# Feed-forward of a quantised transformer block: the transposes of x and h move from TensorE and ScalarE to transposing DMAs on SyncE's queue

## The reference, cut to what matters

```python
def fp4_quant_dequant(x):
    xb = x.reshape(shape[:-1] + (shape[-1] // 16, 16))
    scale = jnp.maximum(jnp.max(jnp.abs(xb), -1, keepdims=True) / 6.0, 1e-12)
    xn = xb / scale
    idx = jnp.searchsorted(_MID, jnp.abs(xn))
    return (_GRID[idx] * jnp.sign(xn) * scale).reshape(shape)

def fp4_linear(x, w):
    return jnp.einsum('bsk,nk->bsn', fp4_quant_dequant(x), fp4_quant_dequant(w))

h = _layernorm(x) * (1 + cb) + sb
gate, y = fp4_linear(h, w_gate), fp4_linear(h, w_up)       # 512 -> 1408
x = x + gb * fp4_linear(silu(gate) * y, w_down)            # 1408 -> 512
```

## Time and profile before

| | |
|---|---|
| median of 3 runs (lowest, highest) | 4354.51 us (4353.13, 4363.64) |
| profiled execution, first to last instruction (span) | 4344.3 us |
| feed-forward's tiles in it, about | 2807 to 4344 us |
| PE busy, whole span | 3769.6 us, 87% |
| DVE busy, whole span | 3500.5 us, 81% |
| ACT, POOL busy | 1612.9 and 1139.1 us |

### The profile page before, as it was taken

One profiled execution on the slowest core, in us unless ns is written; L12 is line 12 of the kernel. 1 busy time (PEld: TensorE's weight loads), 2 busy tenths in 40 slices (PEclk: granted clock), 3 DMA queues, 4 the chain that ended last, 5 costly groups with the idle time before them and its releaser, 6 DMA issues. The chain is left out here.

```text
span 4344.3 us, 155632 instructions
## 1 busy us (share of the span) xinstructions
PE 3769.6 (87%) x65992; PEld 2590.6 (60%) x65992; DVE 3500.5 (81%) x7798; ACT 1612.9 (37%) x3173; POOL 1139.1 (26%) x736
## 2 busy tenths in 40 slices
PE   4888898888898888888888874399999999999999
PEld 3767777676677766777767652145454545545454
DVE  4777788777688776778777757799999999999997
ACT  2434434344353443443434313233333333333333
POOL 1121112211212212112121104433333333333332
PEclk7999999999899998999999986599999999999999
DMA  3000000000000000000000011001111111111100
GB/s 112 13 22 27 23 28 18 23 27 18 23 27 23 27 22 19 27 18 33 18 23 27 13 71 66 15 23 37 31 37 35 33 38 30 37 32 36 38 30 30
DMA packets 73617, 133.45 MB, mean 31 GB/s; under 512 B 13248, under 2 KB 14016, under 8 KB 72896
## 3 DMA queue, kind: packets, MB, share of 16 engines
q1 hardware_dynamic: 72896, 123.13, 8.8%
HBM read 89.56 MB, written 33.55 MB: 28 GB/s over the span
## 5 line engine op out<-in xcount | busy, mean ns | idle before, releaser
L747 POOL TENSOR_TENSOR raw_up<-raw_up,raw_gate 128x1024 f32<-128x1024 f32 x128 | 309.8, 2420 | 1184.1 <-DVE raw_up L797 1184.1
L915 DVE COPY_PREDICATED Am<-pick,banks 128x64 f32<-128x64 uint8 (+2 forms) x1792 | 460.6, 257 | 128.3 <-DVE Am L915 12.6
L1630 PE MATMUL fbank<-dT,hqT 128*128 128x512 f16 x2112 | 490.3, 381 | 21.1 <-ACT hqT L1547 21.1
L1618 PE MATMUL fbank<-gT,xqT 128*128 128x464 f16 (+1 forms) x2304 | 490.1, 363 | 11.4 <-issue 6.6
L1618 PE MATMUL fbank<-uT,xqT 128*128 128x464 f16 (+1 forms) x2304 | 488.3, 362 | 0.0
L526 PE MATMUL banks<-raw_up,raw_gate 128*128 128x256 f32 x2048 | 465.8, 386 | 6.2 <-issue 4.4
L526 PEld LDWEIGHTS banks<-raw_up,raw_gate 128*128 128x128 f32 x2048 | 391.0, 193 | 61.0 <-issue 7.0
L758 POOL TENSOR_TENSOR yrs<-yvar,neg_half 128x32 f32<-128x32 f32 x32 | 174.0, 5437 | 846.0 <-DVE yvar L944 846.0
L1618 PEld LDWEIGHTS fbank<-gT,xqT 128*128 128x128 f16 x2304 | 225.3, 98 | 247.7 <-issue 11.5
L1558 ACT ACTIVATE sil<-fbank,und 128x464 f32<-128x464 f32 (+1 forms) x192 | 124.0, 646 | 656.0 <-PE fbank L1618 656.0
L1618 PEld LDWEIGHTS fbank<-uT,xqT 128*128 128x128 f16 x2304 | 225.6, 98 | 231.7 <-issue 1.3
(11 more groups left out here) (235 smaller groups left out, 8063.1 us busy)
## 6 DMA issues: line engine op xcount, KB each, us to landing
raw_scale<-in_L_attn_x SPq DMA_DIRECT2D x32, 512.0 KB, 3.8
xres<-in_L_attn_x SPq DMA_DIRECT2D x32, 512.0 KB, 3.5
x_after_attention<-xres SPq DMA_DIRECT2D x32, 512.0 KB, 3.6
xl<-x_after_attention SPq DMA_DIRECT2D x64, 256.0 KB, 2.7
xr<-x_after_attention SPq DMA_DIRECT2D x64, 256.0 KB, 2.7
out<-xr SPq DMA_DIRECT2D x64, 256.0 KB, 2.0
raw_gate<-in_L_ffn_w_gate SPq DMA_DIRECT2D x1, 2816.0 KB, 11.5
raw_up<-in_L_ffn_w_up SPq DMA_DIRECT2D x1, 2816.0 KB, 18.7
```

Of the source, the lines that this page charges most:

```text
L747: nc.gpsimd.tensor_tensor(xf[:, j % NXF].rearrange("p g b t -> p (g b) t"), xf[:, j % NXF].rearrange("p g b t -> p (g b) t"), hT[:, :, :, ...
L915: nc.vector.copy_predicated(dst, mask, src).then_inc((done or A_step).sem, 1)
L1618: last = nc.tensor.matmul(GU[2 * pair + t][:, 0:w], xqT[:, u, a, g, :], W[:, b_, g, lo_:hi_], start=(k == 0), stop=(k == 3 * G - 1))
L1630: last = nc.tensor.matmul(DN[1 - u][:], hqT[:, a, kk, :], dT[:, b_, kk, :], start=(first and kk == 0), stop=(end and kk == KF - 1))
```

## The change

The transposes on PE and the copies on ACT go away, with their two PSUM banks. In their place SP issues three transposing DMAs for a tile, from SBUF to SBUF: one for xq (both parts, 128x1024 fp16), one for the high part of hq (128x1408) and one for its low part. hqT gets a second buffer. In SP's stream of body n, the loads of xl (n+2) and xr (n) come first, then the DMA of xq of tile n+1, the two of hq of tile n, and then the store of tile n-1. The down matmuls run in one piece: 22 after the high part has landed, 11 after the low part. The `sem_inc` on turn_go ahead of each DMA carries the wait; nothing waits for turn_go.

```diff
@@ -1337,7 +1336,7 @@
         xq = sb("xq", [P, 2, C], F16)
         hq = sb("hq", [P, 2, I_FF], F16)
         xqT = sb("xqT", [P, 2, 2, G, P], F16)
-        hqT = sb("hqT", [P, 2, KF, P], F16)
+        hqT = sb("hqT", [P, 2, 2, KF, P], F16)
         sil = sb("sil", [P, 2, 480])
         h = sb("h", [P, 2, I_FF])
         mh = sb("mh", [P, I_FF])
...
@@ -1355,8 +1354,9 @@
         Q_STEPS, Q_SCALED = 12, 4
         xgrid_done, hgrid_done = sig("xgrid_done", 1), sig("hgrid_done", 1)
         xlow_done, hlow_done = sig("xlow_done", 1), sig("hlow_done", 1)
-        xT_done, xT_used = sig("xT_done", 1), sig("xT_used", 1)
-        hT_done, hT_used = sig("hTf_done", 4), sig("hTf_used", 4)
+        xT_landed = sig("xT_landed", 1, 16)
+        hT_high, hT_low = sig("hT_high", 1, 16), sig("hT_low", 1, 16)
+        turn_go = sig("turn_go", 3)
         gu_done, sil_done, h_done = sig("gu_done", 3), sig("sil_done", 3), sig("h_done", 3)
         und_done = sig("und_done", 1)
         down_done = sig("down_done", 1)
...
@@ -1417,8 +1417,24 @@
         xstep.per, hstep.per = Q_STEPS, Q_STEPS
 
 
-        def sp_body(sp, j, u, n, do_m, do_out, more):
-            if more:
+        def sp_xT(sp, u, n):
+            after(sp, xq_done, n)
+            after(sp, xlow_done, n)
+            after(sp, gu_done, n - 2)
+            sp.sem_inc(turn_go.sem, 1)
+            sp.dma_start_transpose(xqT[:, u].rearrange("p a g t -> p (a g) t"), xq[:].rearrange("p a n -> p (a n)")).then_inc(xT_landed.sem, 16)
+
+        def sp_hT(sp, u, n):
+            after(sp, hq_done, n)
+            after(sp, down_done, n - 2)
+            sp.sem_inc(turn_go.sem, 1)
+            sp.dma_start_transpose(hqT[:, u, 0], hq[:, 0]).then_inc(hT_high.sem, 16)
+            after(sp, hlow_done, n)
+            sp.sem_inc(turn_go.sem, 1)
+            sp.dma_start_transpose(hqT[:, u, 1], hq[:, 1]).then_inc(hT_low.sem, 16)
+
+        def sp_body(sp, j, u, n, do_m, do_out, more, loads):
+            if loads:
                 after(sp, ln_done, n)
                 b, ts_ = tile_of(j + 1, u)
                 sp.dma_start(xl[:, u], x1[b, ts_, :]).then_inc(xl_loaded[u].sem, 16)
...
@@ -1426,6 +1442,10 @@
                 after(sp, out_stored[u], j - 1)
                 b, ts_ = tile_of(j, u)
                 sp.dma_start(xr[:, u], x1[b, ts_, :]).then_inc(xr_loaded[u].sem, 16)
+            if more:
+                sp_xT(sp, 1 - u, n + 1)
+            if do_m:
+                sp_hT(sp, u, n)
             if do_out:
                 after(sp, out_done, n - 1)
                 jj = j if u else j - 1
...
@@ -1460,7 +1480,7 @@
 
         def dve_hq(dve, u, n):
             after(dve, h_done, n)
-            quantise(dve, n, I_FF, h[:, u], mh[:], q16h, sh, ih, s16h, hp[:, u], hstep, hgrid_done, hq, hq_done, lambda: after(dve, hT_done, n - 1),
+            quantise(dve, n, I_FF, h[:, u], mh[:], q16h, sh, ih, s16h, hp[:, u], hstep, hgrid_done, hq, hq_done, lambda: (after(dve, hT_high, n - 1), after(dve, hT_low, n - 1)),
                      lambda: after(dve, hlow_done, n - 1))
 
         def dve_out(dve, j, u, n):
...
@@ -1558,49 +1560,11 @@
                     nc.scalar.activation(sil[:, pair, 0:hi_ - lo_], GU[2 * pair][:, 0:hi_ - lo_], ACT.Silu, scale=und[:, u, 0:1]).then_inc(sil_done.sem, 1)
                     if s == 0 and more:
                         act_grid(act, n + 1, xstep, hx[:], mx[:], xgrid_done)
-            if do_out:
-                act_hT(act, n - 1, 0)
-                act_hT(act, n - 1, 1, u)
-            if more:
-                act_xT(act, 1 - u, n + 1)
-            if do_out:
-                act_hT(act, n - 1, 2)
             if two_more(n):
                 act_ln(act, u, n + 2)
-            if do_out:
-                act_hT(act, n - 1, 3)
             if do_m:
                 act_grid(act, n, hstep, h[:, u], mh[:], hgrid_done)
...
@@ -1608,7 +1572,7 @@
                     pair = (3 * u + s) % 2
                     w = hi_ - lo_
                     if s == 0:
-                        after(pe, xT_used, n)
+                        after(pe, xT_landed, n)
 
                     after(pe, h_done, n if s >= 2 else n - 1, s - 1 if s >= 2 else s + 2)
                     for t, W in ((0, gT), (1, uT)):
...
@@ -1620,30 +1584,18 @@
                                 k += 1
                     last.then_inc(gu_done.sem, 1)
             if do_out:
-                m = n - 1
-                pe_hT(pe, m, 0, None)
-                pe_hT(pe, m, 1, None, u)
-                if more:
-                    pe_xT(pe, 1 - u, n + 1)
-                def down(ks, a, b_, first=False, end=False):
-                    for kk in ks:
-                        last = nc.tensor.matmul(DN[1 - u][:], hqT[:, a, kk, :], dT[:, b_, kk, :], start=(first and kk == 0), stop=(end and kk == KF - 1))
+                m, v = n - 1, 1 - u
+
+                def down(a, b_, first=False, end=False):
+                    for kk in range(KF):
+                        last = nc.tensor.matmul(DN[v][:], hqT[:, v, a, kk, :], dT[:, b_, kk, :], start=(first and kk == 0), stop=(end and kk == KF - 1))
                     return last
-                after(pe, hT_used, m, 1)
-                down(range(4), 0, 0, first=True)
-                after(pe, hT_used, m, 2)
-                down(range(4, 8), 0, 0)
-                pe_hT(pe, m, 2, None)
-                down(range(8), 0, 1)
-                pe_hT(pe, m, 3, n + 1 if more else (n if do_m else m))
-                after(pe, hT_used, m, 3)
-                down(range(8), 1, 0)
-                after(pe, hT_used, m)
-                down(range(8, KF), 0, 0)
-                down(range(8, KF), 0, 1)
-                down(range(8, KF), 1, 0, end=True).then_inc(down_done.sem, 1)
-            elif more:
-                pe_xT(pe, 1 - u, n + 1)
+                after(pe, hT_high, m)
+                after(pe, scaled_out, m - 2)
+                down(0, 0, first=True)
+                down(0, 1)
+                after(pe, hT_low, m)
+                down(1, 0, end=True).then_inc(down_done.sem, 1)
 
         def run(eng, body, first=None):
 
```

More of the change, by code:

```diff
@@ L1325, in feed_forward @@
         GU = bank[0:4]
-        TR = bank[4:6]
         DN = bank[6:8]
@@ L1449, in dve_xq @@
             after(dve, mod2, n)
-            quantise(dve, n, C, hx[:], mx[:], q16x, sx, ix, s16x, xp[:, u], xstep, xgrid_done, xq, xq_done, lambda: after(dve, xT_done, n - 1),
+            quantise(dve, n, C, hx[:], mx[:], q16x, sx, ix, s16x, xp[:, u], xstep, xgrid_done, xq, xq_done, lambda: after(dve, xT_landed, n - 1),
                      lambda: after(dve, xlow_done, n - 1),
@@ L1505, in pool_xlow @@
         def pool_xlow(pool, n):
-            low_part(pool, n, C, q16x, s16x, xq_done, xq, xlow_done, lambda: after(pool, xT_done, n - 1))
+            low_part(pool, n, C, q16x, s16x, xq_done, xq, xlow_done, lambda: after(pool, xT_landed, n - 1))
         def pool_body(pool, j, u, n, do_m, do_out, more):
@@ L1513, in pool_body @@
             if do_m:
-                low_part(pool, n, I_FF, q16h, s16h, hq_done, hq, hlow_done, lambda: after(pool, hT_done, n - 1))
+                low_part(pool, n, I_FF, q16h, s16h, hq_done, hq, hlow_done, lambda: after(pool, hT_low, n - 1))
             if do_out:
@@ L1529, in act_grid @@
             nc.scalar.activation(m, src, ACT.Abs, bias=grid_shift[:], scale=GRID_SCALE).then_inc(done.sem, 1)
[L1531 to L1547, removed]
         def act_body(act, j, u, n, do_m, do_out, more):
@@ L1622, in pe_body @@
             if do_out:
-                m = n - 1
-                pe_hT(pe, m, 0, None)
-                pe_hT(pe, m, 1, None, u)
-                if more:
-                    pe_xT(pe, 1 - u, n + 1)
-                def down(ks, a, b_, first=False, end=False):
-                    for kk in ks:
-                        last = nc.tensor.matmul(DN[1 - u][:], hqT[:, a, kk, :], dT[:, b_, kk, :], start=(first and kk == 0), stop=(end and kk == KF - 1))
-                    return last
-                after(pe, hT_used, m, 1)
-                down(range(4), 0, 0, first=True)
-                after(pe, hT_used, m, 2)
-                down(range(4, 8), 0, 0)
-                pe_hT(pe, m, 2, None)
-                down(range(8), 0, 1)
-                pe_hT(pe, m, 3, n + 1 if more else (n if do_m else m))
-                after(pe, hT_used, m, 3)
-                down(range(8), 1, 0)
-                after(pe, hT_used, m)
-                down(range(8, KF), 0, 0)
-                down(range(8, KF), 0, 1)
-                down(range(8, KF), 1, 0, end=True).then_inc(down_done.sem, 1)
-            elif more:
-                pe_xT(pe, 1 - u, n + 1)
+                m, v = n - 1, 1 - u
+                def down(a, b_, first=False, end=False):
+                    for kk in range(KF):
+                        last = nc.tensor.matmul(DN[v][:], hqT[:, v, a, kk, :], dT[:, b_, kk, :], start=(first and kk == 0), stop=(end and kk == KF - 1))
+                    return last
```

(9 more changed lines are left out.)

## The result

The changed kernel takes 4303.7 us (median of 7 runs, 4298.6 to 4329.9), the kernel before 4353.1 in the runs beside it. The ratio is 0.9907, interval 0.988 to 0.9935: 0.9% faster, where the prediction said 1.9% slower. It is the first rival, *hidden*, which had a chance of 0.31; the time lies between its two figures (4333 us, and 4279 us if POOL's operations cost DVE nothing). The profiled execution's span is 4301.5 us, 42.8 less than before.

The account below looks back on a forecast made before the run. PE was taken as the bound by a little, DVE right behind. A loss of 1.65 less a gain of 0.42 gives 1.23 us a tile, 76 us over 62 tiles, plus 5 at the ends: 4435 us, range 4285 to 4885.

Parts of the forecast that it names:

- the first rival, *hidden: On SP's queue: L below 2.7 us, xl in time, DVE the bound; 4333 us, or 4279; chance 0.31.
- I take half, 3.5 us: Estimate of L for one part of hq, half of the 7.1 us upper figure; the lower was 2.1 us.
- L: Time from when SP can issue one hq part's transposing DMA until what stands behind it can go; taken as 3.5 us.
- the place where L is paid: SP's queue between hq and xl's load: DVE's statistics wait for xl, 1.65 us a tile.
- The cover of all other DMAs: Before the down matmuls: hq's high part has 9.5 us for 3.5 and a landing, xq 9.3 for 2.6 and a landing.
- DVE stands right behind PE: Feed-forward tile of 23.57 us: PE busy 23.24, DVE 22.27, so taking 2.2 us from PE can't give 2.2.
- the norm's place on ACT: Without the copies ahead, ACT's norm of tile n+2 starts about 3 us earlier, as do POOL's two operations that delay DVE.
- The gain by position: On DVE: POOL's two operations move from L1397 and L1398 to beside L1386 and L1390; 0.42 us a tile, all told.
- the silu's wait: DVE waits 0.16 us for PE's silu of slice 2; claimed as the direct gain of relieving PE.
- The slack of xl: Between xl's landing and DVE's statistics: 1.5 us before the change, used up at L = 2.7 us.
- The prediction's formula: On SP's queue: xl's slack is used up when 3217.05 + 2L + 3.4 passes 3225.80.
- The ends: First transposes of x become a DMA and landing, and the last down matmuls wait for a landing: 5 us more.

Follow-up runs that it names:

- e1: The changed kernel with the low part of hq transposed a second time into an unread spare buffer, right behind the first: 4399.2 us, ratio 1.0134 to the kernel before.
- e2: The changed kernel with the load of xl issued before the two transposing DMAs of hq instead of behind them and the store: 4306.5 us, ratio 0.9915 to before.
- e11: The edits of e1 and e2 together, on the changed kernel: 4306.7 us, ratio 0.9909 to the kernel before.
- e5: The changed kernel without the last 11 of a tile's 33 down matmuls, DMAs and waits kept: 4308.7 us, ratio 0.9895 to the kernel before.
- e3: The changed kernel with ACT's norm of tile n+2 held back until DVE's reciprocal of h's scales: 4351.1 us, ratio 1.0013 to the kernel before.
- e8: e2 plus DVE's statistics of n+2 ahead of quantising x of n+1, and POOL's root ahead of its low part of x: 4262.8 us, ratio 0.9802 to before.
- e4: The kernel before, no transposing DMA, with ACT's norm of tile n+2 moved ahead of the copies of the transposes: 4350.9 us, ratio 1.0011.
- e10: The kernel before, no transposing DMA, with the reordering edits of e8 and e4 and xl loaded first: 4351.3 us, ratio 1.0005.

## Why the prediction was wrong

**The step that failed** is "I take half, 3.5 us" for L. The bounds were 2.1 and 7.1 us and I took a value between them; 1.39 us lies below both. The lower bound was not one: 88 pieces at 0.0235 us is the time that the engines need for the data, and I defined L as the time until what stands behind on the queue can go. The engines do take 24 ns a piece, and SP is free long before, after 1.0 ns a piece. The row taken for the upper end was an issue onto full engines, and the part of it that was back pressure was far more than half. The trace of the kernel before could have said so (timeline of SP's queue): a load of 1 MB in 512 pieces takes 0.45 us to issue as the first of all, with the engines empty, and 2.25 us a little later, with the engines full.

```profile
0.75 0.45 SPq L257 DMA_DIRECT2D kvar<-in_L_wmod  x1
...
9.01 2.25 SPq L255 DMA_DIRECT2D w_v<-in_L_attn_Wv  x1
```

0.45 us for 512 pieces is 0.9 ns a piece, by which 1408 would take 1.2 us, an estimate from a plain load.

**What was right.** Not the direction: that one came with L. But the place where L is paid: e1 adds 1.6 us to the queue and loses 1.27 us a tile, in the wait and at the instruction named; e2 and e11 move xl out of the way and the cost is zero. The cover of all other DMAs: PE waits 1.6 us in 56 tiles for xq. That DVE stands right behind PE, so that 2.2 us taken from PE can't give 2.2 us: e5. That the norm's place on ACT moves POOL's operations and that these lengthen DVE's: e3 takes it back to 23.41 us a tile. One thing stays open: the second buffer of hqT and the down matmuls in one piece came together with the DMAs, and no run takes them apart from the transposes that left PE.

**Sizes.** The gain by position was put at 0.42 us with the silu's wait and measured 0.75 (0.26 of the silu's wait, 0.49 of POOL's), less 0.10 of new wait at L1405. The 0.16 us of the silu's wait was read from one tile; over the tiles its median fell by 0.26. I had L1390 of h waiting 0.4 us where it waits 0.2, and let ACT's grid of h bound L1404, which it does not here. The slack of xl was put at 1.5 us, used up at L = 2.7. The prediction's formula has both DMAs one behind the other; at 1.39 us each, the second waits for POOL's low part (3219.70), so only one L counts, and 3219.70 + 1.39 + 3.4 = 3224.5 would have left 1.3 us. It left 0.7, and nothing in 10 of 56 tiles: from the store's issue to xl's it takes 1.02 us (median), not 0.66, and xl lands in 3.0 us, not 2.8. So the threshold was nearer than I said and L was further below it.

**The ends** were put at 5 us more. Between the first and the last tile's statistics the loop gives 1476.1 - 1443.2 = 32.9 us; the part after the last statistics gives 3.7 us less too (75.8 to 72.2), and the part before them 6.2 less, in which attention's own spread lies. The 10.2 us that were taken as the part outside the first and last instruction are mostly spread between runs: each run's time is 2.0 to 2.1 us above its own span.

The Trainium skill's 261 GB/s (DMA: Bandwidth & Descriptors, Latency and other measured facts) gave an estimate of 1.4 us. The number agrees with the issue by chance: it speaks of the data, which take 2.1 us on each engine and land after 3.5. The 1309 ns that the Trainium skill gives for one 128x128 block (VectorE: DVE Perf Modes, The three transpose paths) do not add up block by block: 11 blocks land in 3.5 us.

The waits of DVE for POOL are as the Trainium skill states them (SBUF — State Buffer, Who interferes with whom): DVE and POOL share a pair of ports as an exclusive lock, a reduction never needs it, and an operation with two inputs in SBUF or in a two-port mode does. The traces agree. L1385 of h, a reduction, takes 1.62 us before, with POOL idle, and in e8, where POOL's norm runs beside it all the time. The 88 columns of L1398 take 0.25 or 1.36 us.

## What to carry to other kernels

Work taken from the engine that sets the pace is worth at most the distance to the next one, here 0.26 of 2.2 us; the rest of the gain came from what the freed engine (ACT) could start earlier. Neither half pays alone: the reordering without the DMAs gives nothing (e4, e10), the DMAs without it nothing that the runs could tell (e3), both together 0.9%, and with DVE's own order made to fit, 2.0% (e8). When an issue is added to a DMA queue, look at the load behind it and at who waits for that load: a load that can be issued a body earlier makes the addition free.

## What the runs showed of the hardware

- A transposing DMA from SBUF to SBUF of 128x1408 fp16 takes 1.38 us of SP's queue and lands 3.5 us after its issue, one of 128x1024 1.25 and 3.1 us (medians). Two of the first kind and one of the second in each tile of 22.9 us raise the engines' share from 0.11 to 0.37.
- The plain DMA issued right behind the two of hq takes 0.72 us of the queue (median) where it took 0.36, and 0.58 in e2. The load of xl behind the DMA of xq in e2 takes 0.36 us, hardly more than the 0.33 it took before.
- Small DVE operations can carry a large wait for POOL inside their own duration (L1398: 0.25 or 1.36 us). The list of waits does not show it, since it counts as busy; only the ends, laid beside POOL's, or the same line at another place do. It goes the other way too: in e8 POOL's one-column product for nmr takes 0.71 us (median) beside DVE's L1390 of x and ends with it, and 0.19 us before and in e2, where DVE is elsewhere (timelines of DVE and POOL in e8):

```profile
3201.41 0.69 DVE L1390 TENSOR_TENSOR hx<-hx,ixf 128x512 f32<-128x512 f32 x1
```

```profile
3201.45 0.71 POOL L1526 TENSOR_TENSOR nmrf<-negmuf,rstdf 128x1 f32<-128x1 f32 x1
```
